# The context of a two-batch cross-attention turned by transposing DMAs instead of by TensorE, its loads reordered, and three steps of batch 0 put first

## What is computed

```
x = x + cross_attention(layernorm(x), ctx, ctx)     # 16 heads of 64, 4096 keys
x = x + hyperbolic_self_attention(layernorm(x))     # 16 heads of 16, 256 keys
x = x + mixture(layernorm(x))                       # 8 experts, best one taken

def cross_attention(query, key, value):
    q, k, v = heads(query @ w_q), heads(key @ w_k), heads(value @ w_v)
    attn = softmax(q @ k.T * 64 ** -0.5)
    return (attn @ v) @ w_o
```

## Time and profile before

| | |
|---|---|
| median of 3 runs | 1123.31 us (1122.32 to 1125.01) |
| the profiled execution's own time | 1124.97 us |
| its span in the trace | 1123.3 us |
| from the start to the first `max_rows` | 49.20 us |
| from there to the second (step 0) | 61.80 us |
| from there to the third (step 1) | 55.04 us |
| PE, DVE, ACT, POOL busy, share of the span | 94%, 72%, 71%, 61% |

### The profile page before, as it was taken

The page is one execution under the profiler, slowest core; times in us unless marked ns, Lnnn a source line. Parts: engine busy times, 40 slices in busy tenths (PEclk is TensorE's granted clock), DMA queues, the critical chain, the costliest instruction groups (busy, mean ns, idle before and its releaser), DMA issues.

```text
span 1123.3 us, 36747 instructions
## 1 busy us (share of the span) xinstructions
PE 1051.4 (94%) x15493; PEld 789.3 (70%) x15493; DVE 810.9 (72%) x1059; ACT 796.4 (71%) x1452; POOL 680.1 (61%) x614
## 2 busy tenths in 40 slices
PE   5899999999999999999999999999999999666688
PEld 3477777777777777777777777777777777543466
DVE  3887777777777777777777777777767759457442
ACT  4776776777777777777777777777776756798854
POOL 3665666666666666666666666676665556734233
PEclk9999999999999999999999999999999999787799
DMA  9100000000000000000000000003000010000000
GB/s 329 51 2 16 7 17 7 17 6 17 7 16 7 17 7 17 7 16 8 17 7 16 8 16 7 16 8 119 7 2 7 28 52 3 2 1 1 1 1 20
DMA packets 27381, 25.45 MB, mean 23 GB/s; under 512 B 1850, under 2 KB 25938, under 8 KB 27218
## 3 DMA queue, kind: packets, MB, share of 16 engines
q1 hardware_dynamic: 27218, 23.10, 6.5%
HBM read 22.57 MB, written 0.52 MB: 21 GB/s over the span
## 4 chain that ended last, share of the span: by engine, by line
PE 81%; DVE 8%; issue 4%; ACT 4%; POOL 2%; DMA 1%; SPq 0%; ACTq 0%; POOLq 0%; DVEq 0%
PE ps L1359 15%; PE ps L1330 14%; PE ps L1443 13%; PE ps L1390 6%; PE ps L1491 5%; PE ps L1486 5%; PE ps L1489 5%; PE ps L1431 4%; PE ps L759 2%; PE ps L719 2%; POOL psums L2048 2%; PE ps L1422 1%; PE ps L1316 1%; DVE m_part L1849 1%; PE ps L535 1%
## 5 line engine op out<-in xcount | busy, mean ns | idle before, releaser
L2048 POOL TENSOR_TENSOR psums<-probs 128x512 f16<-128x512 f32 x512 | 590.1, 1172 | 317.5 <-ACT probs L1686 264.2
L1677 ACT ACTIVATE probs<-ps 128x512 f32<-128x512 f32 x512 | 279.7, 600 | 199.2 <-PE ps L1443 198.3
L1849 DVE TENSOR_REDUCE m_part<-ps 128x2 f32<-128x1024 f32 x256 | 313.2, 1224 | 142.8 <-PE ps L1390 142.7
L1686 ACT ACTIVATE probs<-probs 128x512 f16<-128x512 f32 x384 | 242.1, 632 | 0.3
L1443 PE MATMUL ps<-q_hi,k_p 64*128 64x256 f16 x2048 | 211.1, 269 | 0.0
L1486 PE MATMUL ps<-v_sb,probs 128*128 128x65 f16 x2048 | 205.9, 193 | 4.5 <-POOL psums L2048 4.5
L1489 PE MATMUL ps<-v_sb,probs 128*128 128x64 f16 x2048 | 205.8, 192 | 0.0
L1491 PE MATMUL ps<-v_sb,psums 128*128 128x65 f16 x2048 | 205.4, 194 | 0.0
L1486 PEld LDWEIGHTS ps<-v_sb,probs 128*128 128x128 f16 x2048 | 188.4, 98 | 19.0 <-POOL psums L2048 6.1
L1489 PEld LDWEIGHTS ps<-v_sb,probs 128*128 128x128 f16 x2048 | 188.0, 97 | 15.6
L1491 PEld LDWEIGHTS ps<-v_sb,psums 128*128 128x128 f16 x2048 | 188.2, 97 | 0.0
(11 more groups left out here) (246 smaller groups left out, 1704.4 us busy)
## 6 DMA issues: line engine op xcount, KB each, us to landing
ctx_hi<-in_L_ffn_W_dram SPq DMA_DIRECT2D x2, 2048.0 KB, 9.7
wqk_raw<-in_L_xattn_w_q_dram SPq DMA_DIRECT2D x16, 128.0 KB, 2.3
wqk_raw<-in_L_xattn_w_k_dram SPq DMA_DIRECT2D x16, 128.0 KB, 2.5
probs<-in_ctx_dram SPq DMA_DIRECT2D x4, 512.0 KB, 7.4
wv_raw<-in_L_xattn_w_v_dram SPq DMA_DIRECT2D x16, 128.0 KB, 2.5
k_p<-in_ctx_dram SPq DMA_DIRECT2D x4, 512.0 KB, 9.2
wo_raw<-in_L_xattn_w_o_dram SPq DMA_DIRECT2D x16, 128.0 KB, 2.1
ctx_hi<-in_ctx_dram SPq DMA_DIRECT2D x7, 256.0 KB, 7.0
```

The lines of the kernel that those rows point to most:

```text
L1677: nc.scalar.activation(p_raw[:, s:s + 2, h, :], ps[:, score_bank(n, pair, h), :].rearrange("p (k q) -> p k q", k=2), ACT.Exp, scale=XSCALE ...
L1686: nc.scalar.activation(p_hi[:, s % NP, :, :], p_raw[:, s % NX, :, :], ACT.Copy) \
L1849: nc.vector.tensor_reduce(m_part[:, j, t, :], ps[:, bank:bank + 2, :], AX.X, ALU.max) \
L2048: nc.gpsimd.tensor_tensor(p_lo[:, s % NP, :, :].rearrange("p h q -> p (h q)"), p_raw[:, s % NX, :, :].rearrange("p h q -> p (h q)"), p_hi[ ...
```

## The change

- The context is laid out by chunk: `ctx_hi` and `ctx_lo` become [128, batch, chunk, c, 512]. The products read the same numbers as before.
- The high and low parts are made before turning, from the raw chunk in SBUF, into eight slots `nat` (in the space of `spare`). SyncE then issues one transposing DMA of 128x1024 fp16 for each part of each chunk, 32 in all, each waiting for its part. TensorE's transposes of the context are gone, and with them ScalarE's float copies.
- In the prologue ScalarE makes the high part and GpSimd the low part of batch 0's chunks. In steps 0 and 1, one half chunk of batch 1 a period (table `SPLIT_AT`): ScalarE its high half ahead of the exponentials, VectorE its low half between its two reductions.
- Loads: SyncE loads `x`, the first weights and the first three chunks, ScalarE issues the loads of the other five. Batch 1's loads stand behind the transposing DMAs of batch 0 in SyncE's queue.
- `ORDER` begins with (0,0), (1,0), (2,0), then (0,1), (1,1), (2,1), and goes on as before. Batch 1 is first projected at the end of step 1. Six of its transposing DMAs stand in SyncE's queue ahead of step 2's loads and ten ahead of step 3's.
- In the prologue TensorE projects chunk `j+1` before the maxima of chunk `j`. `tail_constants` comes before the first chunk. One bank of PSUM, which the transposes used to write first, is set to zero by VectorE. The low part of the keys (L1840, now L1869) stays on VectorE.

The diff, cut:

```diff
-ORDER = tuple((i // 2, i % 2) for i in range(STEPS - 6)) + tuple(
+ORDER = tuple((hp, b) for b in range(B) for hp in range(3)) + tuple((i // 2, i % 2) for i in range(6, STEPS - 6)) + tuple(
     (hp, b) for b in range(B) for hp in range(HP - 3, HP))
+FIRST1 = 3
-TURNED = 2
-EARLY = 2
-LATER_AT = {q: q + EARLY for q in range(KCH - EARLY)}
+EARLY = 0
+BY_SP = 3
+SPLIT_AT = {g: (KCH + EARLY + g // 2, g % 2) for g in range(2 * (KCH - EARLY))}
+NAT = 8
+LEAD = 4
...
+        def split_context_high(act, i, halves=(0, 1)):
+            b, u = divmod(i, KCH)
+            if b == 0:
+                act.wait_ge(s_ctx[u], 16)
+            else:
+                act.wait_ge(s_raw[u], 32)
+            if i >= NAT:
+                act.wait_ge(s_dh[i % NAT], 16)
+            parts = raw_parts(i)
+            for raw, tiles in [parts[h] for h in halves if h < len(parts)]:
+                last = nc.scalar.activation(nat_part(i, 0, tiles), raw, ACT.Copy)
...
+        def split_context_low(eng, ops, i, halves=(0, 1)):
...
+                last = ops.tensor_tensor(nat_part(i, 1, tiles), raw, nat_part(i, 0, tiles), ALU.subtract)
...
+            def turn_context(i, low):
+                b, u = divmod(i, KCH)
...
+                sp.dma_start((ctx_hi, ctx_lo)[low][:, b, u, :, :].rearrange("p c (t k) -> p (c t) k", t=CS),
+                             nat[:, i % NAT, low, :], transpose=True).then_inc((s_dh, s_dl)[low][i % NAT], 16)
+
+            turn_context(0, 0)
+            for u in range(1, KCH + 1):
+                if u < KCH:
+                    turn_context(u, 0)
+                turn_context(u - 1, 1)
+                if u == 3:
+                    load_wv(0, 0)
+                    load_wqk(1, ORDER[1][0])
+            for u in range(KCH):
+                load_context(u)
...
             for n in range(STEPS):
+                if n == FIRST1 - 1:
+                    for u in range(3):
+                        turn_context(KCH + u, 0)
+                        turn_context(KCH + u, 1)
+                if n == FIRST1:
+                    for u in range(3, KCH):
+                        turn_context(KCH + u, 0)
+                        turn_context(KCH + u, 1)
                 step(n)
...
+            def project_first_k(j, part):
+                if part == 0:
+                    at_least(pe, s_kl, j - 1)
...
+                    pe.wait_ge(s_dh[j], 16)
...
+                pe.wait_ge(s_dl[j], 16)
...
             pe.wait_ge(s_const, 3)
-            transposes_ctx(0)
             transposes_x()
-            project_first_k(0, PV)
-            transposes_ctx(1)
+            project_first_k(0, 0)
             pe.wait_ge(s_xc, NC)
             project_q(0, 0, 0)
-            for j in range(2, KCH + 2):
-                transposes_ctx(j)
...
+            project_first_k(0, 1)
+            for j in range(KCH):
+                if j + 1 < KCH:
+                    for part in range(2):
+                        project_first_k(j + 1, part)
+                maxima(2 * j, 0, 0)
+                maxima(2 * j + 1, 0, 0)
...
-                    if first and q in LATER_AT:
-                        transposes_later(q, LATER_AT[q], 0)
...
             split_k(0, 0)
-            context(0)
+            for u in range(BY_SP, KCH):
+                act.dma_start(*first_context(u)).then_inc(s_ctx[u], 16)
+                if u == BY_SP + 1:
+                    split_context_high(act, 0)
+            split_context_high(act, 1)
```

More of the change, by code:

```diff
@@ new lines, in nat_part, with first_context @@
+        def nat_part(i, low, tiles):
+            return nat[:, i % NAT, low, :].rearrange("p (c t k) -> p t c k", c=NC, t=CS)[:, tiles, :, :]
+        first_chunks = ctx.rearrange("b (n p t) c -> b n p t c", p=P, t=8)
+        def first_context(u):
+            tiles = slice(4 * (u % 2), 4 * (u % 2) + 4)
+            return stage[u // 4][:, u // 2 % 2, tiles, :], first_chunks[0, u // 2, :, tiles, :]
+        def split_context_high(act, i, halves=(0, 1)):
+            b, u = divmod(i, KCH)
+            if b == 0:
+                act.wait_ge(s_ctx[u], 16)
+            else:
+                act.wait_ge(s_raw[u], 32)
[4 more added lines that the diff above has]
+                last = nc.scalar.activation(nat_part(i, 0, tiles), raw, ACT.Copy)
+            if 1 in halves:
+                last.then_inc(s_th, 1)
+            else:
+                last.then_inc(s_t2, 1)
@@ new lines, in split_context_low @@
+        def split_context_low(eng, ops, i, halves=(0, 1)):
+            if 1 in halves:
+                eng.wait_ge(s_th, i + 1)
+            else:
+                eng.wait_ge(s_t2, i - KCH - EARLY + 1)
+            if i >= NAT:
+                eng.wait_ge(s_dl[i % NAT], 16)
+            parts = raw_parts(i)
+            for raw, tiles in [parts[h] for h in halves if h < len(parts)]:
+                last = ops.tensor_tensor(nat_part(i, 1, tiles), raw, nat_part(i, 0, tiles), ALU.subtract)
+            if 1 in halves:
+                last.then_inc(s_tl if i < KCH + EARLY else s_t3, 1)
@@ L1233, in _, with load_context, low_done @@
             load_wqk(0, 0)
[L1234 to L1241, removed]
+            for u in range(BY_SP):
+                sp.dma_start(*first_context(u)).then_inc(s_ctx[u], 16)
+            def load_context(u):
                 for i in range(2):
-                    to = last_raw[:, 2 * i:2 * i + 2, :] if u == KCH - 1 else raw1[i][:, :, u + 1, :]
+                    to = last_raw[:, 2 * i:2 * i + 2, :] if u == KCH - 1 else raw1[i][:, u + 1, :, :]
                     first = 4 * (u % 2) + 2 * i
                     sp.dma_start(to, chunks[1, u // 2, :, first:first + 2, :]).then_inc(s_raw[u], 16)
+            def turn_context(i, low):
+                b, u = divmod(i, KCH)
+                def low_done(i):
+                    if i < KCH + EARLY:
+                        sp.wait_ge(s_tl, i + 1)
+                    else:
+                        sp.wait_ge(s_t3, i - KCH - EARLY + 1)
+                if low:
+                    low_done(i)
+                else:
+                    sp.wait_ge(s_th, i + 1)
+                    if b == 1 and u >= 1:
+                        low_done(i - 1)
+                sp.dma_start((ctx_hi, ctx_lo)[low][:, b, u, :, :].rearrange("p c (t k) -> p (c t) k", t=CS),
[10 more added lines that the diff above has]
+                load_context(u)
             def load_experts(w):
@@ L1534, in step @@
                     pv_before(n, q, (0, 1))
-                    if first and q in LATER_AT:
-                        transposes_later(q, LATER_AT[q], 1)
                     if q == Y_IN and 0 < n < STEPS - 2:
@@ L1707, in step @@
                         take_v(0, n + 1, MX)
-                    if first and q in LATER_AT:
-                        context_later(LATER_AT[q], 0)
                     if n == DONE0 and q in TURN_IN:
@@ L1714, in step @@
                     high(n, s + 3)
-                    if first and q in LATER_AT:
-                        context_later(LATER_AT[q], 1)
                     if q == OT_IN and not first:
```

184 lines of the change are left out of this document (65 added, 119 removed).

## The result

The change makes the kernel slower, by a third of a per cent: 1125.56 us in the median of 17 runs (1122.59 to 1129.19) against 1122.32 of 17 runs of the kernel before (1119.69 to 1125.01). The ratio is 1.0033, with a 95% interval from 1.0023 to 1.0042. Forecast were 1117.6 us and a gain. The profiled execution has a span of 1124.9 us, 1.6 more than before.

A forecast was written before the change was run, and what follows sets the result against it. TensorE was taken to bound the steps, VectorE most of the prologue. The terms -5.5 - 0.5 + 1.0 - 0.2 - 0.5 gave -5.7 us, from the median 1123.31 to 1117.6 us, range 1113 to 1123.

The forecast's parts named there:

- Its own signs: First `max_rows` at 48.5 us, second 55.8 to 56.8 behind; wrong if under 4 us closer or prologue over 3 off.
- TensorE's transposes in step 0: Periods 0 to 5 of step 0: eight transposes a period leave TensorE's path, -5.5 us.
- The first period's wait: Step 0's first period: TensorE's wait behind VectorE's low part of the context shrinks, between nothing and 0.7, taken as -0.5 us.
- The low halves on VectorE: Steps 0 and 1: a subtraction between two reductions in each of 16 periods just fits its gap, +1.0 us.
- rival 4: Steps 0 and 1: low halves delay VectorE's second reduction 0.7 us every period, +11, 1128 us; chance 0.04.
- The price of a transposing DMA: Prologue: 1.2 us for each transposing DMA, taken from the side of a plain DMA of that size.
- Rivals 2 and 3: Rival 2: DMAs from 2.4 us slow the prologue, 1129 at 2.75, chance 0.11; rival 3: blocks singly, about 1340, 0.02.
- rival 1: Prologue: transposing DMAs at 1.6 to 2.4 us each set its pace, 1117 to 1123 us; chance 0.16.
- my far end: Transposing DMA's highest price: each row of 128 fp16 numbers a packet at 43 ns, 2.75 us a DMA.
- The prologue's start: First reduction at 22.5 us, five transposing DMAs running beside and behind the loads from about 15.5, -0.2 us.
- The prologue's pace: VectorE's work in the prologue stays; it gains some idle time before reductions, -0.5 us.
- Rival 5: Prologue: TensorE's clock falls to 1.2 GHz, making the prologue 8 us longer, 1125 us; chance 0.03.

The follow-up runs named there:

- e_before2: The kernel before the change, unchanged, profiled again; `max_rows` at 48.53 and 108.72 us.
- e_both: The changed kernel with the edits of e_tail and e_act together; 1120.49 us, ratio to before 0.9988.
- e_third: e_both with a third transposing DMA a chunk in the prologue, batch 1's loads waiting for these; 1128.34 us, ratio 1.0058.
- e_ring: e_both with only the first context load in SyncE's queue, ScalarE issuing the other seven; 1120.73 us, ratio 0.9986.
- e_late: e_both with the loads of chunks 5 to 7 issued behind the high part of chunk 3; 1119.51 us, ratio 0.9979.
- e_act: The changed kernel with ScalarE's high part of chunk 3 put ahead of its copy of the first query; 1123.15 us, ratio 1.0005.
- e_tail: The changed kernel with the second step's query projection and its low part back ahead of the last chunk's maxima; 1123.54 us, ratio 1.0008.
- e_after2: The changed kernel, unchanged, profiled again; `max_rows` at 54.80 and 112.81 us.
- e_hybrid2: e_hybrid with step 0's last low half behind both reductions; 1117.57 us, ratio to before 0.9953.
- e_hybrid: The changed kernel with batch 0 turned by TensorE and loaded as before, batch 1 still by DMAs; 1118.0 us, ratio to before 0.9956.

## Why the prediction was wrong

Its own signs failed: the prologue is 6 us off (54.57 for 48.5), and step 0 is 3.8 us closer and not 4. The sum was -5.7 us; against the second profile of before the profile of the change has +3.8. By the traces that is +3.7 for the prologue's start, +0.6 for its pace, +1.8 for its end, -4.2 for step 0 without the late start and the clock, +1.0 for the late start and +1.0 for the clock. Point by point:

- **TensorE's transposes in step 0, -5.5: right.** In e_before2 TensorE is busy for 56.59 us of step 0, in e_both for 51.29, so 5.3 less, and the clock fell in neither. But step 0 became only 4.2 us shorter (60.19 and 56.03): TensorE's idle time in it grew by 1.1, from 3.60 to 4.74.
- **The first period's wait, -0.5: wrong.** It grew by 0.5 us. TensorE's longest wait there, in e_before2 and then in e_both (engine, line, what it waited for, us, times, longest):

```profile
PE ps L1390 <- DVE ctx_lo L1864: 1.0, 1, 1.0
```

```profile
PE ps L1441 <- DVE k_p L1870: 1.5, 1, 1.5
```

  The keys' parts come later than before; in e_both's chain of waits ScalarE's high half stands ahead of the exponentials with 0.62 us, which the prediction named and let reduce the gain by 0.2 only.
- **The low halves on VectorE, +1.0: near in size, in part by luck.** They take 0.68 to 0.72 us in most periods and fit their gap, and rival 4 did not come. But the forecast had 0.06 in each of 16 periods. In step 1 they cost 0.0; most of the cost is one instance, in step 0's last period, which comes late behind the tables and takes 1.36 us. `project_k` waits 0.5 us for VectorE there, and 0.2 us more of TensorE's idle time lie in the periods before: about 0.7.
- **The price of a transposing DMA, 1.2 us: right**, at 1.3 to 1.37 us. e_third agrees with a threshold between two and three a chunk. Rivals 2 and 3 did not come, and rival 1 did not as I put it. Each row of 256 bytes is about a packet, as my far end had it, but a packet took 4.4% (10.2 + 0.7 - 6.5) of 16 engines over 1124.9 us by 32000, so 25 ns and not 43.
- **"The prologue's start", -0.2: the step that failed worst, by 3 us** (25.68 for 22.5). What failed is the overlap: I let five transposing DMAs run "beside and behind" the loads from 15.5 us on and gave TensorE's part 1 us. Beside the loads the first one alone landed only at 19.5, with the engines full (share 0.99 to 1.24 from 10 to 22 us). The loads, and five at 1.37, bring 15.5 + 6.9 = 22.4; with the products behind that 23.4; e_both, where nothing else is in the way, has 24.46. The first product took 0.63 us and the later ones 0.38, though the trace grants the clock at 1.00 there; why stays open. Neither e_ring nor e_late bought the start back by another order of loads, which fits work of the full engines and not a wait in a queue. That no order can is not shown.
- **"The prologue's pace", -0.5: the wait was left out.** I asked what each engine has to do and not in which order ScalarE's list has it. In the change ScalarE stood 7.5 us before the query with chunk 3's high part behind it. Of VectorE's waits of 1.43 and 2.15 us all but 1.14 came of that (e_act). In e_both VectorE's run from first to last reduction is 24.7 us, 1.5 less than before: the gain was there and larger than the 0.5 forecast, but in the change the waits made it +0.6.
- **The prologue's end was no term at all.** The prediction lists what went and came but not that the second step's projections moved behind the last maxima; the code of the change shows it. It cost 2.8 us: 1.8 before `max_rows`, made longer by the lower clock, and 1.0 before step 0's first product (e_tail).
- **Rival 5, the clock**, came in part and as a consequence: TensorE fell to 1.2 GHz where it had waited for late chunks, which made the end longer, and again in step 0's last period, 1.0 us; in e_both it kept 2.4 GHz through prologue and step 0 with the same work. The prediction also read step 0's 61.80 us as it stood, with the earlier trace rows granting a clock of 0.97 in it; the sum does not rest on that, its signs (4 us closer, 55.8 to 56.8) do.
- **A slip in the working:** with the low halves at +3.5 the forecast's own range ends at 1120.1, not 1120.5.

The time came out above the range because the range held only prices of the DMA and the low halves: the waits in the engines' lists, and the loads' hold on the first transposing DMA, were not in it. The Trainium skill, "Advanced Engine Details and Errata", section "X-Bar Transpose (TRN2)", puts transposing DMAs level with ordinary ones, 350 to 400 GB/s. The trace does not agree: 198 GB/s with full engines against 359 for the loads. By either figure two a chunk stay under VectorE's 3.2 us, so that the forecast would have been as wrong.

## What to carry to other kernels

A stage that is bound by one engine gains nothing from work taken off another, but it loses by every wait that the new order puts in front of its engine: write down each queue's order, and for each wait what is queued behind it. Put a transposing DMA where the DMA engines are idle and the engine it relieves is the bound (here from step 0 on), and leave it out where loads fill them and something waits for the first. When a rewritten loop drops a step that used to stand inside it, look at what follows the loop's last turn. Before two traces are compared stage by stage, look at the granted clock of each stage: a fall of 1.0 to 1.6 us in one period was as large here as what was looked for.

## What was not expected of the hardware

- A transposing DMA of 128x1024 fp16, SBUF to SBUF, takes 1.23 us or more of SyncE's issuing (a plain one mostly 0.4 to 0.5), lands 3.0 us after its issue at the earliest and moves 198 GB/s with all 16 DMA engines full. Beside all loads of batch 0 the longest landed after 9.8 to 12.3 us, in e_late, with three loads put off, after 7.6.
- GpSimd's subtraction, with both its inputs in SBUF, holds up VectorE's normalisation of `x`. In the change it begins at 9.25 us, while VectorE is at it; in the repeat, e_after2, at 10.38, when VectorE is done. The four instructions, in the change and then in e_after2:

```profile
8.40 3.19 DVE L1836 TENSOR_SCALAR xn<-x_sb,mv,rstd 128x256 f32<-128x256 f32 x4
```

```profile
8.60 1.38 DVE L1836 TENSOR_SCALAR xn<-x_sb,mv,rstd 128x256 f32<-128x256 f32 x4
```

  One took 2.2 us in the change; before and in e_after2 none was over 0.41. TensorE's transposes of `x` start at 11.74 us and not, as in e_after2, at 10.13. It cost nothing there: TensorE waited until 19.61 for the first transposing DMA, and in e_after2 the first reduction was no earlier.
- TensorE's clock falls or not in the same stall of step 0 (last period, some 2 us without work): it did in one of two profiles of the kernel before, in both of the changed one, in e_late and in e_hybrid2, not in e_tail, e_act, e_both and e_hybrid. It cost 1.6 us before and 1.0 in the change. Most of the spread between runs of one kernel may come from such places; that was not tried.
